# The second LoRA product on two halves of TensorE's array, in two turns

## What is computed

```python
base_out = jnp.einsum('bti,oi->bto', x, W) + b
A = lora_As[adapter_mapping]
Bm = lora_Bs[adapter_mapping]
lora_h = jnp.einsum('bti,bir->btr', x, A)
lora_out = jnp.einsum('btr,bro->bto', lora_h, Bm)
return base_out + lora_out * SCALING
```

## Time and profile before

| | |
|---|---|
| median of 3 runs | 992.07 us (991.67 to 992.74) |
| the profiled execution's own time | 994.31 us |
| its span | 992.6 us |
| TensorE busy | 982.7 us (99%) |
| VectorE busy | 586.8 us (59%) |
| ScalarE busy | 464.9 us (47%) |
| GpSimd busy | 256.0 us (26%) |

### The profile page before, as it was taken

The page is one execution under the profiler, slowest core; times in us unless marked ns, Lnnn a source line. Parts: engine busy times, 40 slices in busy tenths (PEclk is TensorE's granted clock), DMA queues, the critical chain, the costliest instruction groups (busy, mean ns, idle before and its releaser), DMA issues.

```text
span 992.6 us, 14042 instructions
## 1 busy us (share of the span) xinstructions
PE 982.7 (99%) x4787; PEld 830.4 (84%) x4787; DVE 586.8 (59%) x969; ACT 464.9 (47%) x854; POOL 256.0 (26%) x244
## 2 busy tenths in 40 slices
PE   9999999999999999999999999999999999999998
PEld 7888888878888888888888888888888998888876
DVE  5654586777784323596423398333377587785762
ACT  4645567555661333572333373233356273535342
POOL 5242232654400631400532230261140450000000
PEclk9999999999999999999999999999999999999999
DMA  8997866666977877867887777986688740615222
GB/s 287 334 327 281 309 216 245 240 231 236 340 265 260 283 229 193 274 222 267 287 278 193 233 249 248 321 279 192 192 293 285 254 166 28 228 61 194 78 93 85
DMA packets 121486, 230.12 MB, mean 232 GB/s; under 512 B 12612, under 2 KB 12612, under 8 KB 121160
## 3 DMA queue, kind: packets, MB, share of 16 engines
q1 hardware_dynamic: 118880, 220.81, 66.5%
q0 software_dynamic: 2400, 8.41, 2.3%
q10 hardware_dynamic: 136, 0.01, 0.0%
HBM read 165.74 MB, written 63.44 MB: 231 GB/s over the span
## 4 chain that ended last, share of the span: by engine, by line
PE 96%; DVE 1%; ACT 1%; issue 1%; DMA 0%; SPq 0%; ACTq 0%; DVEq 0%
PE bank L1820 95%; PE bank L1844 1%; PE bank L1981 1%; DMA w_raw<-in_w 0%; ACT xs_hi L1126 0%; ACT bank L1277 0%; DVE hg L1644 0%; DVE t_lo L1535 0%; DVE greater L1624 0%; ACT res L1285 0%; DVE diff L1601 0%; DVE top L1597 0%; DVE wins L1620 0%; DVE rank L1627 0%; DVE greater L1618 0%
## 5 line engine op out<-in xcount | busy, mean ns | idle before, releaser
L1820 PE MATMUL bank<-cop_hi,wring 128*128 128x512 f32 x1234 | 380.8, 389 | 0.9 <-ACT bank L1041 0.9
L1820 PEld LDWEIGHTS bank<-cop_hi,wring 128*128 128x128 f32 x1234 | 231.8, 188 | 49.4 <-ACT bank L1041 1.3
L1820 PE MATMUL bank<-cop_lo,wring 128*128 128x512 f32 x616 | 239.8, 389 | 0.0
L1820 PE MATMUL bank<-op_hi,wring 128*128 128x512 f32 x560 | 173.8, 389 | 0.0
L1472 DVE TENSOR_TENSOR v<-bank,p7s 128x512 f32<-128x512 f32 x44 | 30.4, 692 | 204.6 <-PE bank L1820 204.6
L1820 PEld LDWEIGHTS bank<-cop_lo,wring 128*128 128x128 f32 x616 | 115.7, 188 | 23.8
L1820 PEld LDWEIGHTS bank<-op_hi,wring 128*128 128x128 f32 x560 | 105.2, 188 | 21.7
L1820 PE MATMUL bank<-op_lo,wring 128*128 128x512 f32 x280 | 109.0, 389 | 0.0
L1072 ACT ACTIVATE s<-bank 128x512 f32<-128x512 f32 x44 | 26.3, 598 | 117.9 <-PE bank L1820 117.8
L1458 DVE TENSOR_TENSOR op_lo<-h,op_hi 128x512 fp32r<-128x512 f32 x100 | 72.9, 747 | 3.3 <-ACT op_hi L1029 3.1
L821 POOL TENSOR_TENSOR h_t<-h,h 128x512 f32<-128x512 f32 x20 | 27.7, 1385 | 161.1 <-DVE h L1494 161.1
(11 more groups left out here) (227 smaller groups left out, 1931.4 us busy)
## 6 DMA issues: line engine op xcount, KB each, us to landing
wring<-wgu_scratch SPq DMA_DIRECT2D x231, 256.0 KB, 3.1
wring<-wd_scratch SPq DMA_DIRECT2D x140, 256.0 KB, 4.9
wgu_scratch<-wring SPq DMA_DIRECT2D x77, 256.0 KB, 3.5
x_raw<-in_x SPq DMA_DIRECT2D x32, 256.0 KB, 6.2
c_scratch<-c_out SPq DMA_DIRECT2D x32, 256.0 KB, 2.9
c<-c_scratch SPq DMA_DIRECT2D x32, 256.0 KB, 4.6
xs_raw<-x_scratch SPq DMA_DIRECT2D x16, 512.0 KB, 6.2
out<-res SPq DMA_DIRECT2D x32, 256.0 KB, 2.1
```

Of the source, the lines that this page charges most:

```text
L1820: return e.matmul(out_ap, lhs, rhs, start=start, stop=stop, skip_group_check=True)
```

## The change

`cond_lora` now uses the array as two halves of 64 rows (`PART`). The upper four sequences of a group have rows 0 to 63 and its first 128 tokens (`PT`), the lower four rows 64 to 127 and the other 128. Each half multiplies its 64 rows with its own 128 tokens. The halves write to different banks at a time: in turn 0 half 0 writes banks 0 and 1 and half 1 banks 2 and 3, in turn 1 the other way round. Each turn has 24 products of 128 columns in pairs. Turn 1 waits (`pe_turn`) for the last product of turn 0.

```diff
+    PART = 64
+    NPART = P // PART
+    PT = GT // NPART
...
         def cond_base(t, m, k):
...
+            return mm3(acc[m][:, :], w0_hi[:, k, m * P:(m + 1) * P], w0_lo[:, k, m * P:(m + 1) * P],
+                       xa_hi[t % 2][:, k, :], xa_lo[t % 2][:, k, :], k == 0, k == KC - 1)
...
+        def cond_lora(t, turn):
+
+
+            s, own = t % 2, KC // NPART
+            if turn == 0:
+                e.wait_ge(lh_lo_done, t + 1)
+                e.wait_ge(b_lo_done, NG * (t + 1))
+            else:
+                e.wait_ge(pe_turn, (NPART - 1) * t + turn)
+            for c in range(own):
+                for g in range(NG):
+                    for b_, h_ in ((b_hi[s], lh_hi[s]), (b_hi[s], lh_lo[s]), (b_lo[s], lh_hi[s])):
+                        for i in range(NPART):
+                            m = (i + turn) % NPART * own + c
+                            rows, tok = slice(i * PART, (i + 1) * PART), slice(g * GT + i * PT, g * GT + (i + 1) * PT)
+                            done = mm(acc[m][:, tok], b_[rows, g, m * P:(m + 1) * P], h_[rows, tok], False, False)
+            if turn + 1 < NPART:
+                done.then_inc(pe_turn, 1)
```

The order of a tile changes with it, and `pe_acc` goes up by four once, at the tile's end:

```diff
         for t in range(NT):
...
+            else:
+                turn_a(t)
+                for m in range(KC):
                     e.wait_ge(c_closed, nth(t - 1, m))
-                    for k in range(KC):
+                    if m == KC - 1:
+                        lora_in(t)
+                    for k in range(KC - 1):
                         if m == 0:
                             e.wait_ge(x_lo, nth(t, k))
                         cond_base(t, m, k)
...
+            cond_base(t, 3, KC - 1)
+            cond_base(t, 2, KC - 1)
+            cond_lora(t, 0)
+            cond_base(t, 1, KC - 1)
+            cond_lora(t, 1)
+            cond_base(t, 0, KC - 1).then_inc(pe_acc, KC)
```

More of the change, by code:

```diff
@@ L289, in build @@
     pool_late_hi, pool_late = sem("pool_late_hi"), sem("pool_late")
-    warm_done = sem("warm_done")
+    pe_turn = sem("pe_turn")
     gs_done, g_hi_done, g_lo_done = sem("gs_done"), sem("g_hi_done"), sem("g_lo_done")
@@ L1661, in route_h @@
                                 ALU.add).then_inc(dve_freed, 1)
-        e.memset(plain(warm[:, :]), 0.0).then_inc(warm_done, 1)
+        linked(e.memset(plain(warm[:, :]), 0.0))
         e.wait_ge(pool_const, 1)
@@ L2057, in out_h2 @@
                 False, True).then_inc(pe_acc, 1)
-        e.wait_ge(warm_done, 1)
+        e.wait_ge(dve_chain, 1)
         for _ in range(9):
             mm(ring[3][:, :], warm[:, 0:P], warm[:, :], True, True)
-        for k in range(KC):
[L2063 to L2070, removed]
-        for t in range(NT):
-            for m in range(KC):
-                if t > 0:
+        for t in range(NT):
+            if t == 0:
+                for k in range(KC):
+                    e.wait_ge(x_lo, nth(0, k))
+                    e.wait_ge(w0_lo_done, k + 1)
+                    if k == 2:
+                        turn_a(0)
+                    if k == KC - 1:
+                        lora_in(0)
+                    else:
+                        for m in range(KC):
+                            cond_base(0, m, k)
+            else:
+                turn_a(t)
+                for m in range(KC):
                     e.wait_ge(c_closed, nth(t - 1, m))
-                    for k in range(KC):
+                    if m == KC - 1:
+                        lora_in(t)
+                    for k in range(KC - 1):
                         if m == 0:
```

## The result

The changed kernel takes 1003.3 us (median of 4 runs, 1001.65 to 1004.75), the kernel before 992.4 in the same runs; the ratio is 1.0108, 95% interval 1.0089 to 1.0128. The sign was right, the size was not: forecast was 1025.6. What happened is, in its mechanism and nearly to the digit, the first rival (1003.5): the halves run side by side.

The account below looks back on a forecast made before the run. TensorE bounds the kernel (busy 982.7 of 992.6 us), every new wait paid in full. LoRA products 21.1, shape changes 5.8 and waits 6.6 make +33.5 us on 992.07: 1025.6 us, range 997 to 1038.

Parts of the forecast that it names:

- the first rival: LoRA products: both halves load and multiply at once, a pair in one step, -1.0 us; total 1003.5 us; chance 0.30.
- The products: LoRA products in each tile: 48 half-array products one after the other, 0.110 to 0.120 us each, +21.1 us; chance 0.50.
- Changes of shape: Switches between full and half array, four a tile, 32 in all: 0.18 us each, +5.8 us, range 0 to 11.
- Waits: New TensorE waits from the new order, at tile starts, in tiles 0 and 7 and leaving the stage: +6.6 us together.
- Tile 0: First tile: only 6 base products, before 12, lie ahead of the LoRA products, so TensorE waits on lh_lo: +1.3 us.
- Tile starts: Start of each later tile: the load behind the c_out wait isn't made ahead, +0.2 us x 7 = +1.4 us.
- Tile 7: Last tile: the long chain to lh_lo moves by 2.17 us, so TensorE waits on it: +1.9 us.
- Leaving: End of the first stage: the gate products wait for the first closing copy, +1.1 us with the load.
- L1041: Leaving the stage: ScalarE's copy, wanted after 12 products, ends at 153.8 while TensorE is there at 152.9: +0.9 us.
- The gathers: Gathered rows for the transposes, wanted 2.75 us sooner: hidden with 2.6 us to spare, uncovered if LoRA gets no dearer.
- pe_turn: Wait between turns in a tile: costs nothing, as three base products (0.69 us) cover some 0.3 us.
- The rest of the kernel: From the first gate product on: as long as before.

Follow-up runs that it names:

- order-alone kernel: Changed kernel with its order, single closing and wait between turns, but the kernel before's 24 full-array LoRA products of 256 columns: 999.9 us, ratio 1.0062.
- one-block kernels: Kernel before with half-array LoRA products, both turns in one block after all base products: 997.31 us; the second also moves transposes to the tile's start: 998.6 us.
- 64-weight kernel: Changed kernel, each LoRA product with 64 of its 128 weight columns: 997.35 us.
- the quarters: First of the one-block kernels with products of 32 rows and 64 tokens, four at a time, full waits between turns, all banks closed at the end: 1023.02 us.
- 256-column pair: Changed kernel, each half-array product over all 256 tokens of its group: 1006.24 us.
- the first experiment: Changed kernel, in each turn all 12 products of half 0 issued first, then all 12 of half 1: 1027.1 us.
- 64-column kernel: Changed kernel, each LoRA product only over the first 64 of its 128 tokens: 1004.65 us.

## Why the prediction was wrong, point by point

- **The products: the step that failed.** +21.1 us was "each of the 48 products costs 0.110 to 0.120"; it measured 24 x 0.112 - 2.88 = -0.19 a tile, -1.5 in all. The unit was right (0.112, also for full products), and so was the reason that columns don't set it. The step from "once per product with its load" to "one for the whole array" was not drawn from a row: the loads of one array that overlap in the earlier trace rows say nothing on two halves. That the trace showed no two at once was no evidence, since the kernel before issues none. The Trainium skill's rule (TensorEngine Tiling (Array Packing), Key Properties: different tiles load and multiply in parallel) holds here, with a pair at 0.112 us. It deserved more than 0.30.
- **Side by side is not faster by itself.** The rival's -1.0 us measured -1.5. That halves at a common pace gain nothing was the part of the argument that carried the sign.
- **Changes of shape.** 32 x 0.18 = 5.8 us; measured 0.68 / 4 = 0.17 each, 5.4 us. The middle between 0 and 0.34 came out, but it was taken for want of a nearer row, so this is luck; 0.34, forecast as the most that one change could cost, is what entry and exit take together.
- **Waits.** Forecast 6.6; the same terms measured 4.5. Tile 0: 1.3, measured 0.9. Tile starts: 0.2, measured 0.14 each. Tile 7: 1.9, measured 1.24. Leaving: 1.1, measured 0.9; L1041, forecast at +0.9, cost 0.5, and a later wait of 0.9 on it that was there before is gone. The gathers, called hidden with 2.6 us to spare in the forecast's own case and uncovered in the shorter tile, did show: 1.1 us in two tiles.
- **pe_turn** cost nothing, as forecast.
- **The rest of the kernel was to stay as long.** It did within 0.4 us, but for the third stage. At 967.22 TensorE waits 1.89 us, as it did before at 959.19 (1.93), and behind it the granted clock is 0.83 where it was 1.00; the stage is 1.6 us longer, and all of it is lost within 5 us of that wait.

The same two stretches, changed kernel first (stretch, TensorE, its loads, VectorE, ScalarE, GpSimd, granted clock, DMA share, GB/s):

```profile
970.00:975.00 5.00, 5.00 (x20) 4.04 (x19) 1.11 (x5) 1.00 (x3) 0.00 (x0) 0.83 0.00 0
```

```profile
962.00:967.00 5.00, 5.00 (x23) 4.14 (x23) 2.12 (x10) 1.39 (x3) 0.00 (x0) 1.00 0.00 0
```

That is not the change's doing in any way that I can show: of 15 later executions of the kernel before, 9 have a mean clock of 0.997 or 0.998 and the others 0.999 or 1.000, and the changed kernel's four have 0.998 or 0.999. The same fall at the same place stands in the profiled executions of the order-alone kernel, both one-block kernels, the 64-weight kernel and the quarters, and not in those of the other five, four of which have halves. Whether the changed kernel is hit more often stays open; it is at most 2 us of the 11.

## What to carry to other kernels

Before cutting a product into halves of the array, ask what sets the step of one product: if it is the load of its weights, the halves run side by side, each at the full price of that load, and half of the rows and half of the columns buy next to nothing (here 0.19 us of 2.88 a tile). What got cheaper here was the product with fewer weight columns. By an estimate from the 256-column pair (0.118 us, where 512 columns on the full array take 0.229) a product whose moving columns outlast its load would, too; no such kernel was run. Each switch between full array and halves costs 0.17 us on average (0.14 going in, 0.20 coming out), and reordering to make room for it can cost as much as the halves themselves: here 4.5 of the 8.4 us in the first stage came with the new order.

## What the runs showed that I had not expected

- Halves, and quarters of 32 rows, start within 0.01 us of each other and keep their own pace: two or four loads of 128 columns in 0.112 us.
- The products of one half run ahead of earlier ones of the other, by three products in the first experiment.
- TensorE's front end put out products with their loads at 0.016 us each (pairs at 0.032).
- A wait of 0.8 us behind a block of quarters was followed by 1.2 GHz behind every block (the 12 base products there take 4.2 to 5.3 us for 2.8), while the changed kernel's waits of 0.8 to 1.2 us in this stage kept 2.4 GHz. The 64-column kernel lost clock in mid-stage (granted 0.52 from 80 to 87 us) with waits no longer than those. The runs don't tell which property of the block made the difference.
